# Unread products in the history stage of a recommender kernel, and a table moved to another PSUM bank

## The chip, the cores and the metric

The kernel runs on one core of a Trainium2 chip. Its metric is the device time of one execution in microseconds (us). A core has five engines with an instruction stream each: TensorE (PE in the rows, with PEld for its loads of the stationary operand), VectorE (DVE), ScalarE (ACT), GpSimd (POOL) and SyncE (SP). They meet only in semaphores: `then_inc` raises one, `wait_ge` holds an engine until one has reached a value.

## The reference

2048 examples have an item, a user and 100 users of a history. A row of a table has D = 128 numbers. The tables have 12500 and 62500 rows, and the ids are drawn from a wider range: an id past the end reads the last row, which is what most ids of the history do.

```python
items_emb = item_table[items]
user_emb = user_table[users]
hist_emb = user_table[history_users]
scores = einsum('bhd,bd->bh', hist_emb, user_emb)
user_his_emb = einsum('bh,bhd->bd', scores, hist_emb)
x = concatenate([items_emb, user_his_emb, user_emb], axis=1)   # 2048 x 384
x = dice(batchnorm(x @ W1 + b1, g1, be1), a1)                  # W1: 384 x 1024
x = dice(batchnorm(x @ W2 + b2, g2, be2), a2)                  # W2: 1024 x 512
return x @ W3 + b3                                             # W3: 512 x 1
```

Everything is in float32. A float32 product of 128x128 by 128x128 stands in the trace as two MATMUL records and two LDWEIGHTS records. A transpose is one of each.

## The kernel before

**Plan (0 to 45 us).** The 2048 examples are ordered by how many ids of their history are past the end, and cut into `TILES` = 16 tiles of 128 with about equal counts in a tile. `rank` holds each example's place in that order, one column per tile. Ids past the end need no gather: their count times the last row's score and the last row itself enter as one product. The ids left are gathered in slots: a slot is one row for each of the 128 examples of a tile. Four slots are a group (`GROUP` = 4), and a ring of 16 rows in SBUF holds four groups. `ends` holds the running count of slots. Examples are put in their order by products with matrices of zeros and ones ("places"), which VectorE builds by comparing `rank` with column numbers (`find_places`, L689, `find_own_places`, L697 and L702).

**History stage (45 to 838 us).** The four engines run the same loop over tiles and groups, each in its own stream:
- GpSimd gathers a group's four slots (L520, an indirect DMA each). Ahead of a group it waits for the indices (`idx_ready`) and for the place in the ring (`rows_free`). The arrival of a group is passed on to VectorE (`relay`) behind the third gather of the next.
- VectorE (`weigh`) multiplies the rows with the user's row (L812), sums over D (L818), masks the score (L822), and hands on the next indices (L827).
- ScalarE scales each slot's row by its score (`scale_rows`, L1236) into one of four buffers `scaled`. It waits for the scores of the group and, for each buffer, for TensorE's sum four slots before (`slot_summed`). The last scale of a group raises `rows_free`. Behind the loop over groups of a tile stands `keep_rows` (L1205), which waits for the placing product of two tiles ahead and copies it; then come the tile's last group and `pooled_T` (L1265). VectorE sorts a tile's ids out of what L1205 copied.
- TensorE sums the scaled rows in PSUM by products with the identity (`add_rows`, L1486), four a group, each waiting for its scale. Between groups it does other work of the tile, written out by hand: the last row's product (L1495), two transposes (L1502, L1503), `place_own` (L1423, L1428), `layer1_pooled` of the tile before (L1473), `place_keys` of two tiles ahead, the first half behind group 1 and the second behind the loop (L1407), and `layer1_own` (L1467), half behind group 2 and half behind group 3. The loop over the groups that are left (L1522) holds `add_rows` alone.

A tile has seven or eight groups: four ahead of the loop, two or three in it, one behind. A tile's order of work on TensorE is thus: last row, group 0, transposes, places, layer 1 of the tile before, group 1, places, group 2, half of layer 1, group 3, half of layer 1, rounds, the placing product, last group.

**Dense stage (838 to 1014 us).** Batchnorm, dice, W2, again batchnorm and dice, W3. TensorE is busy 95% of it.

`keep_busy` (L1453 to L1456) multiplies the identity by itself into the first 128 columns of PSUM bank 0, and nothing reads these. The kernel before calls it twice: 8 products ahead of the last tile's last group, and 20 behind the last `layer1_pooled`. `warm_up` (L1386) is the same in the plan.

Of the kernel before, what the change touches and what calls it, by code (L numbers as in the profile page):

```python
# [6 lines left out]
P = 128  # L7
# [31 lines left out]
def recommender_kernel(nc, items, users, history, item_table, user_table, W1, b1, g1, be1, a1,  # L39
# [6 lines left out]
    TILES = B // P  # L46
# [18 lines left out]
    BINS = HIGH - LOW + 1  # L65
# [7 lines left out]
    with ExitStack() as ctx:  # L73
# [153 lines left out]
        ps = ctx.enter_context(nc.psum_tensor("ps", [P, 8, 512], F32))  # L227
# [6 lines left out]
        ids_in = ps[:, 1, 64:64 + 2 * TILES]  # L234
        lasts = ps[:, 1, 96:96 + TILES]
        lasts_cut = ps[:, 1, 112:112 + TILES]
        rank = ps[:, 0, 2 * P:2 * P + TILES]
        rank_bins = ps[:, 1, 144:144 + TILES]
        same = ps[:, 1, 256:512].rearrange("p (t u) -> p t u", u=TILES)

# [146 lines left out]
        def hold(eng, semaphore, value):  # L387
            if not isinstance(value, int):
                eng.wait_ge(semaphore, value)  # L389
                eng.sem_inc(passed, 1)  # L390
            elif value > 0:
                eng.wait_ge(semaphore, value)

        def end_of(eng, t):

            return eng.value_load(ends[0:1, t + 1:t + 2], min_val=MIN_SLOTS * (t + 1), max_val=HIST * (t + 1))
# [977 lines left out]
        def _(pe):  # L1374
# [22 lines left out]
            def place_keys(t, j):  # L1397

                if t:
                    pe.wait_ge(places_found, 2 * t + 3 + j)  # L1400
                if j == 0 and t:
                    pe.wait_ge(tile_kept, t)
                    pe.wait_ge(whose_kept, t)
                for m in range(M1):
                    if t == 0 and m % 4 == 0:
                        pe.wait_ge(places_found, 2 * j + m // 4 + 1)
                    mm = nc.tensor.matmul(rows_ps, places[:, m, j, :], people[:, 2 * m + j, :],  # L1407
                                          start=(j == 0 and m == 0), stop=(j == 1 and m == M1 - 1), skip_group_check=True)
                if j == 1:
                    mm.then_inc(rows_placed, 1)  # L1410

            def place_own(i, t):

                pe.wait_ge(own_places_found[i], t + 1)
                if t == 0:
                    hold(pe, own_moved[i], own_more[i] + 1)
                elif i == 0:
                    pe.wait_ge(user_kept, t)
                    pe.wait_ge(item_set, t)
                of = own_ps[:, i * D:(i + 1) * D]  # L1420

                def first(s):
                    return nc.tensor.matmul(of, own_places[i][:, s, :], own_rows[i][:, s, :], start=(i == 0 and s == 0),  # L1423
                                            stop=(i == 1 and s == OWN_SLOTS - 1), skip_group_check=True)
                first(0)
                with pe.Fori(0, own_more[i]) as s:
                    hold(pe, more_found[i], own_more[i] * t + s + 1)
                    nc.tensor.matmul(of, more_places[i][:, :], own_rows[i][:, bass.ds(s + OWN_SLOTS, 1), :], start=False, stop=False,  # L1428
                                     skip_group_check=True).then_inc(more_used[i], 1)
                for s in range(1, OWN_SLOTS):  # L1430
                    mm = first(s)
                mm.then_inc(own_placed[i], 1)
# [20 lines left out]
            def keep_busy(count):  # L1453

                for _ in range(count):
                    nc.tensor.matmul(idle_ps, ident[:, :], ident[:, :], start=True, stop=True)  # L1456

            def layer1_own(t, blocks):


                if blocks.start == 0:
                    pe.wait_ge(both_kept, t + 1)
                if t:
                    pe.wait_ge(l1_kept, M1 * (t - 1) + blocks.stop)
                for m in blocks:
                    for k, of in ((0, P), (2, 0)):
                        nc.tensor.matmul(l1_ps[:, m, :], w1[:, k, m * P:(m + 1) * P], both_T[:, of:of + P],  # L1467
                                         start=(k == 0 and m == blocks.start), stop=False, skip_group_check=True)

            def layer1_pooled(t):  # L1470
                pe.wait_ge(pooled_kept, t + 1)
                for m in range(M1):
                    mm = nc.tensor.matmul(l1_ps[:, m, :], w1[:, 1, m * P:(m + 1) * P], pooled_T[:, :],  # L1473
                                          start=False, stop=True, skip_group_check=True)
                    if m % 4 == 3:
                        mm.then_inc(l1_done, 1)

            def add_rows(g, t, end):
                for j in range(GROUP):
                    if j < GROUP - 1:  # L1480
                        hold(pe, slot_scaled, g * (GROUP - 1) + (t * (GROUP - 1) + j + 1))
                    elif end:
                        pe.wait_ge(end_scaled, t + 1)
                    else:
                        hold(pe, rows_free, g + 1)
                    nc.tensor.matmul(pooled_ps, scaled[:, j, :], ident[:, :], start=False, stop=False,  # L1486
                                     skip_group_check=True).then_inc(slot_summed, 1)

            for t in range(TILES):
                begin.append(end_of(pe, t))  # L1490
                g0, g1 = begin[t] >> 2 if t else 0, begin[t + 1] >> 2
                pe.wait_ge(last_ready, t + 1)
                if t:
                    pe.wait_ge(pooled_kept, t)
                nc.tensor.matmul(pooled_ps, last_scaled[:, :], ident[:, :], start=True, stop=False,  # L1495
                                 skip_group_check=True)
                add_rows(g0, t, False)
                pe.wait_ge(user_kept, t + 1)
                pe.wait_ge(item_set, t + 1)
                if t:  # L1500
                    pe.wait_ge(both_kept, t)
                nc.tensor.transpose(turn_ps[:, 0:P], own[:, 0, :], ident[:, :])  # L1502
                nc.tensor.transpose(turn_ps[:, P:2 * P], own[:, 1, :], ident[:, :]).then_inc(turned, 1)  # L1503
                if t + 1 < TILES:
                    place_own(0, t + 1)
                if t:
                    layer1_pooled(t - 1)
                add_rows(g0 + 1, t, False)
                if t + 1 < TILES:
                    place_own(1, t + 1)  # L1510
                if t == 0:
                    place_keys(1, 0)
                    place_keys(1, 1)
                elif t + 2 < TILES:
                    place_keys(t + 2, 0)
                add_rows(g0 + 2, t, False)
                layer1_own(t, range(0, 4))
                add_rows(g0 + 3, t, False)
                if t == 0:
                    place_keys(2, 0)  # L1520
                layer1_own(t, range(4, M1))
                with pe.Fori(g0 + 4, g1) as g:  # L1522
                    add_rows(g, t, False)
                if t + 2 < TILES:
                    place_keys(t + 2, 1)
                if t == TILES - 1:
                    keep_busy(8)
                add_rows(g1, t, True)
                pe.wait_ge(slot_summed, g1 * GROUP + (t * GROUP + 2 * GROUP))
                pe.sem_inc(pooled, 1)  # L1530
# [181 lines left out]
```

## Time and profile before

| | |
|---|---|
| median of 3 runs | 1004.77 us (1000.77 to 1005.12) |
| the profiled execution | 1015.52 us, span 1013.7 us |
| busy in the span | TensorE 653.8, VectorE 522.8, GpSimd 495.0, ScalarE 360.5 us |
| gathers of history slots | 432 records (L520), 412.1 us |
| sums of scaled rows (L1486) | 984 records, 211.7 us |

The rows further down are of the profiled execution. A row of the timeline is one piece of work or several equal ones behind each other (x4); the bracket says how long the engine was idle ahead of it and what ended that. "issue" means that nothing in the profile was waited for; "remote" that the semaphore was raised by something the profile could not assign. The granted clock (PEclk) is TensorE's, as a share of its full 2.4 GHz, and has two levels, so 0.70 is a mixture of stretches at full and at half speed.

### The profile page before, as it was taken

The numbers are of one execution on the slowest core, as the hardware profiler recorded it, in microseconds if no ns is written. First come the engines' busy times: TensorE is split into PE (matmuls) and PEld (weight loads), VectorE is DVE, ScalarE is ACT, GpSimd is POOL, SyncE is SP. The second block draws the span as 40 slices with busy tenths as digits, with TensorE's granted clock in tenths as the row PEclk, the third lists the DMA queues.
The fourth block names the chain that finished last, engine by engine and source line by source line (L and its number), as shares of the span: only waits on it lengthen the run. The fifth ranks groups of instructions, "written<-read, shape, count | busy, mean of one in ns | idle before, by whom it ended". The sixth has DMA issues, their size and how long they took to land.

```text
span 1013.7 us, 17230 instructions
## 1 busy us (share of the span) xinstructions
PE 653.8 (64%) x3753; PEld 606.6 (60%) x3753; DVE 522.8 (52%) x1353; ACT 360.5 (36%) x884; POOL 495.0 (49%) x561
## 2 busy tenths in 40 slices
PE   4563665637473846566566475756665569999998
PEld 3552555537373736465566364745664469888887
DVE  7653444344353625353445254544434536999758
ACT  3122232322231414132223142332233247787556
POOL 6655544545455453636354635545544524290036
PEclk8676776767587666767677667768777779999999
DMA  7111111111111111111111111111111110000000
GB/s 215 40 38 39 37 34 35 37 37 37 37 35 39 30 44 25 44 27 44 30 40 32 44 26 39 36 32 39 38 34 35 42 22 1 2 1 0 1 1 2
DMA packets 17241, 34.65 MB, mean 34 GB/s; under 512 B 8104, under 2 KB 8400, under 8 KB 17168
## 3 DMA queue, kind: packets, MB, share of 16 engines
q0 software_dynamic: 14208, 29.13, 11.7%
q1 hardware_dynamic: 2960, 4.67, 1.4%
q8 instruction: 32, 0.52, 0.2%
q14 instruction: 41, 0.34, 0.1%
HBM read 33.76 MB, written 0.01 MB: 33 GB/s over the span
## 4 chain that ended last, share of the span: by engine, by line
PE 45%; another core or an unknown queue 19%; issue 18%; ACTq 8%; ACT 6%; DVE 3%; DVEq 0%; PEldq 0%; POOL 0%; POOLq 0%
PE ps L1486 14%; PE ps L1544 10%; PE ps L1407 6%; PE ps L1423 5%; ACTq L1236 3%; ACT scaled L1236 3%; PE ps L1473 3%; ACTq L1257 2%; PE ps L1495 1%; ACTq L389 1%; ACTq L390 1%; PE ps L1559 1%; PE ps L1428 1%; PE ps L1386 1%
## 5 line engine op out<-in xcount | busy, mean ns | idle before, releaser
L520 POOL DMA_INDIRECT rows<-in_L_rec_user_table_dram,slot_idx x432 | 412.1, 954 | 388.3 <-ACT scaled L1236 260.6
L1486 PE MATMUL ps<-ident,scaled 128*128 128x128 f32 x984 | 211.7, 381 | 225.8 <-ACT scaled L1236 171.9
L1486 PEld LDWEIGHTS ps<-ident,scaled 128*128 128x128 f32 x984 | 186.8, 278 | 249.4 <-issue 221.8
L1236 ACT ACTIVATE scaled<-rows,work 128x128 f32 (+1 forms) x492 | 176.5, 401 | 271.5 <-remote 191.1
L812 DVE TENSOR_TENSOR prod<-rows,ps 128x512 f32<-128x512 f32 x122 | 83.7, 686 | 168.4 <-POOLq L527 88.1
L689 DVE SCALAR_TENSOR_TENSOR h<-ps,col_no 128x1024 f32<-128x1024 f32 (+1 forms) x34 | 39.2, 1161 | 159.0 <-ACT ranked L1205 88.1
L1544 PE MATMUL ps<-h,w 128*128 128x256 f32 (+1 forms) x576 | 113.3, 356 | 1.0 <-DVE h L1042 1.0
L1407 PE MATMUL ps<-wide,h 128*128 128x104 f32 x512 | 98.6, 369 | 14.6 <-issue 14.6
L1544 PEld LDWEIGHTS ps<-h,w 128*128 128x128 f32 x576 | 99.6, 190 | 12.8 <-issue 1.2
L1407 PEld LDWEIGHTS ps<-wide,h 128*128 128x128 f32 x512 | 94.3, 281 | 21.2 <-issue 21.2
L818 DVE TENSOR_REDUCE work<-prod 128x512 f32 (+1 forms) x122 | 83.7, 686 | 38.8 <-issue 25.5
L1467 PE MATMUL ps<-both_T,w 128*128 128x128 f32 x512 | 72.2, 292 | 22.7 <-issue 22.7
L1467 PEld LDWEIGHTS ps<-both_T,w 128*128 128x128 f32 x512 | 67.6, 209 | 18.3 <-issue 18.1
L1224 ACT ACTIVATE h<-ps,par 128x128 f32<-128x128 f32 x128 | 36.4, 372 | 106.0 <-remote 103.6
L1423 PE MATMUL ps<-wide,work 128*128 128x128 f32 x160 | 33.2, 306 | 41.2 <-issue 41.2
L1205 ACT ACTIVATE ranked<-ps 128x104 f32<-128x104 f32 x16 | 4.1, 258 | 138.3 <-remote 114.2
L1423 PEld LDWEIGHTS ps<-wide,work 128*128 128x128 f32 x160 | 26.3, 215 | 40.3 <-issue 40.1
L556 POOL TENSOR_SCALAR h<-h,scale,shift 128x256 f32<-128x256 f32 (+1 forms) x29 | 22.2, 779 | 49.4 <-DVE h L1042 28.8
L822 DVE SCALAR_TENSOR_TENSOR work<-wide,ends_f,work (+1 forms) x122 | 27.2, 223 | 33.9 <-issue 16.4
L1423 PE MATMUL ps<-wide 128*128 128x128 f32 x160 | 34.1, 364 | 4.8 <-DVE wide L697 4.8
L1423 PEld LDWEIGHTS ps<-wide 128*128 128x128 f32 x160 | 32.2, 285 | 4.9 <-issue 4.9
L1473 PE MATMUL ps<-pooled_T,w 128*128 128x128 f32 x256 | 33.3, 286 | 0.5 <-ACT pooled_T L1265 0.5
(217 smaller groups left out, 784.7 us busy)
## 6 DMA issues: line engine op xcount, KB each, us to landing
rows<-in_L_rec_user_table_dram,slot_idx POOLq DMA_INDIRECT x432
w<-in_L_rec_W_dram SPq DMA_DIRECT2D x1, 2048.0 KB, 17.5
w<-in_L_rec_W_dram SPq DMA_DIRECT2D x1, 1536.0 KB
h<-in_r_history_users_dram SPq DMA_DIRECT2D x2, 400.0 KB, 3.4
wide<-in_L_rec_user_table_dram,own_idx POOLq DMA_INDIRECT x5
wide<-in_L_rec_item_table_dram,own_idx POOLq DMA_INDIRECT x5
last_row<-in_L_rec_user_table_dram SPq DMA_DIRECT2D x1, 64.0 KB
last_item<-in_L_rec_item_table_dram SPq DMA_DIRECT2D x1, 64.0 KB
```

The source lines that it names most:

```text
L520: nc.gpsimd.indirect_dma_start(rows[:, s, :], None, user_table, bass.IndirectOffsetOnAxis(slot_idx[:, s:s + 1], 0)).then_inc(landed[s], 16)
L689: nc.vector.scalar_tensor_tensor(places[:, of, j, :], rank.rearrange("p (m j) -> p m j", j=2)[:, of, j].unsqueeze(2).to_broadcast(shape), ...
L812: nc.vector.tensor_tensor(prod[:, :, :], rows[:, at, :], user_now.unsqueeze(1).to_broadcast([P, GROUP, D]), ALU.mult).then_inc(multiplied, 1)
L818: nc.vector.tensor_reduce(raw[:, pair], prod[:, :, :], AX_X, ALU.add).then_inc(dotted, 1)
L1224: nc.scalar.activation(h1[:, m, t * P:(t + 1) * P], l1_ps[:, m, :], ACT.Identity, bias=b1c[:, m:m + 1]).then_inc(l1_kept, 1)
L1236: nc.scalar.activation(scaled[:, j, :], rows[:, bass.ds((g & (GROUPS - 1)) * GROUP + j, 1), :], ACT.Copy, scale=score[:, bass.ds(g * GROUP ...
L1407: mm = nc.tensor.matmul(rows_ps, places[:, m, j, :], people[:, 2 * m + j, :], start=(j == 0 and m == 0), stop=(j == 1 and m == M1 - 1), sk ...
L1423: return nc.tensor.matmul(of, own_places[i][:, s, :], own_rows[i][:, s, :], start=(i == 0 and s == 0), stop=(i == 1 and s == OWN_SLOTS - 1 ...
L1467: nc.tensor.matmul(l1_ps[:, m, :], w1[:, k, m * P:(m + 1) * P], both_T[:, of:of + P], start=(k == 0 and m == blocks.start), stop=False, sk ...
L1473: mm = nc.tensor.matmul(l1_ps[:, m, :], w1[:, 1, m * P:(m + 1) * P], pooled_T[:, :], start=False, stop=True, skip_group_check=True)
L1486: nc.tensor.matmul(pooled_ps, scaled[:, j, :], ident[:, :], start=False, stop=False, skip_group_check=True).then_inc(slot_summed, 1)
L1544: mm = nc.tensor.matmul(l2_ps[c % 2][:, o, 0:w], w2[:, k, o * P:(o + 1) * P], h1[:, k, chunk(c)], start=(k == 0), stop=(k == M1 - 1))
```

## The change

Two things. The rank columns move from PSUM bank 0 (columns 256 to 271) to bank 4, behind the table `in_bin`; they are written and read by the same VectorE instructions as before. And TensorE gets unread products (`keep_busy`): 40 in a loop of its own ahead of the first tile's first product, 4 behind each half of `layer1_own` in each tile, 10 in each round of the loop over groups, and 4 behind the placing product in the tiles that have one there.

```diff
--- before.py
+++ after.py
@@ -234,7 +234,7 @@
         ids_in = ps[:, 1, 64:64 + 2 * TILES]
         lasts = ps[:, 1, 96:96 + TILES]
         lasts_cut = ps[:, 1, 112:112 + TILES]
-        rank = ps[:, 0, 2 * P:2 * P + TILES]
+        rank = ps[:, 4, BINS * TILES:(BINS + 1) * TILES]
         rank_bins = ps[:, 1, 144:144 + TILES]
         same = ps[:, 1, 256:512].rearrange("p (t u) -> p t u", u=TILES)
 
@@ -1486,9 +1486,16 @@
                     nc.tensor.matmul(pooled_ps, scaled[:, j, :], ident[:, :], start=False, stop=False,
                                      skip_group_check=True).then_inc(slot_summed, 1)
 
+
+
+            BETWEEN = 4
+            IN_LOOP = 10
             for t in range(TILES):
                 begin.append(end_of(pe, t))
                 g0, g1 = begin[t] >> 2 if t else 0, begin[t + 1] >> 2
+                if t == 0:
+                    with pe.Fori(0, 10):
+                        keep_busy(4)
                 pe.wait_ge(last_ready, t + 1)
                 if t:
                     pe.wait_ge(pooled_kept, t)
@@ -1515,14 +1522,18 @@
                     place_keys(t + 2, 0)
                 add_rows(g0 + 2, t, False)
                 layer1_own(t, range(0, 4))
+                keep_busy(BETWEEN)
                 add_rows(g0 + 3, t, False)
                 if t == 0:
                     place_keys(2, 0)
                 layer1_own(t, range(4, M1))
+                keep_busy(BETWEEN)
                 with pe.Fori(g0 + 4, g1) as g:
                     add_rows(g, t, False)
+                    keep_busy(IN_LOOP)
                 if t + 2 < TILES:
                     place_keys(t + 2, 1)
+                    keep_busy(BETWEEN)
                 if t == TILES - 1:
                     keep_busy(8)
                 add_rows(g1, t, True)
```

The first place is TensorE's stream where the history stage begins; `ends` is the load of the tile's end, `last_scaled` the last row times its weight. Before:

```order
L1423 MATMUL ps<-wide,work 128x128 x4
L396 TENSOR_LOAD ends [waits w1_loaded,plan_ready]
L396 ISA x2
L1495 MATMUL ps<-ident,last_scaled 128x128 [waits last_ready]
L1486 MATMUL ps<-ident,scaled 128x128 [waits slot_scaled] x3
L1486 MATMUL ps<-ident,scaled 128x128 [waits rows_free]
L1502 MATMUL ps<-ident,own 128x128 [waits item_set,user_kept]
```

The same stretch now:

```order
L396 TENSOR_LOAD ends [waits w1_loaded,plan_ready]
L396 ISA x2
L1497 UNCONDITIONAL_BRANCH
L1456 MATMUL ps<-ident 128x128 x4
L1497 REGISTER_ALU
L1497 COMPARE_AND_BRANCH
L1502 MATMUL ps<-ident,last_scaled 128x128 [waits last_ready]
L1486 MATMUL ps<-ident,scaled 128x128 [waits slot_scaled] x3
```

Ten rounds of four products stand between the load of `ends` and the wait for the last row (L1495 before is L1502 now).

The second place is the loop over groups and what follows it, in TensorE's stream; `h1` in L1407 holds the places of the second half. Before:

```order
L1467 MATMUL ps<-both_T,w1 128x128 x8
L1522 UNCONDITIONAL_BRANCH
L1522 ISA
L1486 MATMUL ps<-ident,scaled 128x128 [waits slot_scaled]
L389 REGISTER_ALU
...
L1486 MATMUL ps<-ident,scaled 128x128 [waits rows_free]
L1522 ISA
L1522 COMPARE_AND_BRANCH
L1407 MATMUL ps<-wide,h1 128x104 [waits places_found]
L1407 MATMUL ps<-wide,h1 128x104 x7
```

The same stretch now (L1531 is the loop's line):

```order
L1467 MATMUL ps<-both_T,w1 128x128 x8
L1456 MATMUL ps<-ident 128x128 x4
L1531 UNCONDITIONAL_BRANCH
L1531 ISA
...
L1486 MATMUL ps<-ident,scaled 128x128 [waits rows_free]
L1456 MATMUL ps<-ident 128x128 x10
L1531 ISA
L1531 COMPARE_AND_BRANCH
L1407 MATMUL ps<-wide,h1 128x104 [waits places_found]
L1407 MATMUL ps<-wide,h1 128x104 x7
L1456 MATMUL ps<-ident 128x128 x4
```

Each product here is two loads and two products in the engine's stream. The loop's round grows by ten products behind its four sums, and four more stand on either side of the loop and its placing product. The streams of the other engines are as before.

## Rows read from the trace of the kernel before

**Rows 1.** Windows of the two stages: start:end, length, busy of PE, PEld, DVE, ACT, POOL, clock, DMA, GB/s.
```profile
45.00:838.00 793.00, 467.38 (x2656) 438.18 (x2655) 348.58 (x1020) 228.32 (x689) 399.92 (x421) 0.70 0.14 36
838.00:1014.00 176.00, 167.16 (x998) 150.44 (x998) 144.00 (x241) 121.77 (x171) 65.67 (x89) 0.99 0.00 1
```
**Rows 2.** The page's chain of waits by engine, shares of the span.
```profile
PE 45%; another core or an unknown queue 19%; issue 18%; ACTq 8%; ACT 6%; DVE 3%; DVEq 0%; PEldq 0%; POOL 0%; POOLq 0%
```
**Rows 3.** List of waits: engine, line, waited for, us in total, times, longest.
```profile
POOL rows L520 <- ACT scaled L1236: 260.6, 48, 9.1
ACT scaled L1236 <- remote: 191.1, 38, 10.1
...
ACT ranked L1205 <- remote: 114.2, 13, 11.7
```
**Rows 4.** The page's costliest groups: busy us, mean ns, idle before.
```profile
L1486 PE MATMUL ps<-ident,scaled 128*128 128x128 f32 x984 | 211.7, 381 | 225.8 <-ACT scaled L1236 171.9
```
**Rows 5.** Timeline of 305 to 336 us: start, duration, engine, line, count, idle before.
```profile
306.01 0.95 POOL L520 DMA_INDIRECT rows<-in_L_rec_user_table_dram,slot_idx  x1 [0.30 <-issue]
...
309.23 1.44 ACT L1236 ACTIVATE scaled<-rows,work 128x128 f32 x4 [10.10 <-remote]
...
309.78 4.92 PE L1486 MATMUL ps<-ident,scaled 128*128 128x128 f32 x20 [7.02 <-ACT scaled L1236]
311.09 1.44 ACT L1236 ACTIVATE scaled<-rows,work 128x128 f32 x4 [0.42 <-PE ps L1486]
311.48 0.95 POOL L520 DMA_INDIRECT rows<-in_L_rec_user_table_dram,slot_idx  x1 [4.51 <-ACT scaled L1236]
...
317.87 0.46 PE L1486 MATMUL ps<-ident,scaled 128*128 128x128 f32 x2 [2.46 <-issue]
...
318.17 3.62 PE L1407 MATMUL ps<-wide,h 128*128 128x104 f32 x16
...
325.23 0.95 POOL L520 DMA_INDIRECT rows<-in_L_rec_user_table_dram,slot_idx  x1 [0.30 <-issue]
328.82 0.26 ACT L1205 ACTIVATE ranked<-ps 128x104 f32<-128x104 f32 x1 [11.09 <-remote]
...
329.98 2.05 PE L1486 MATMUL ps<-ident,scaled 128*128 128x128 f32 x8 [8.20 <-ACT scaled L1236]
```
**Rows 6.** Timeline of 286 to 298 us, TensorE.
```profile
291.30 0.25 PE L1407 MATMUL ps<-wide,h 128*128 128x104 f32 x1 [1.18 <-issue]
```
**Rows 7.** Windows of the three bursts of the tile, columns as in rows 1.
```profile
282.50:289.90 7.40, 6.63 (x53) 6.58 (x51) 5.12 (x18) 1.89 (x5) 5.88 (x6) 0.89 0.18 44
297.30:308.50 11.20, 5.45 (x47) 5.26 (x45) 5.53 (x16) 1.64 (x5) 7.53 (x8) 0.96 0.19 48
311.50:327.70 16.20, 7.56 (x34) 6.71 (x33) 2.89 (x9) 2.58 (x7) 11.32 (x12) 0.71 0.19 49
```
**Rows 8.** Chain of waits near 840 us, unread products of the kernel before.
```profile
840.19 4.47 PE ps L1456 x40
```
**Rows 9.** Timeline of the plan and the first tile.
```profile
10.62 4.33 PE L1386 MATMUL ps<-not_before,ident 128*128 128x128 f32 x20 [3.51 <-issue]
...
44.63 0.80 PE L1495 MATMUL ps<-ident,last_scaled 128*128 128x128 f32 x2 [5.85 <-issue]
...
49.35 1.92 PE L1423 MATMUL ps<-wide 128*128 128x128 f32 x8
...
58.38 0.38 ACT L1252 ACTIVATE both_T<-ps 128x256 f32<-128x256 f32 x1 [11.36 <-remote]
```
**Rows 10.** Timeline of 660 to 682 us, a tile with two rounds.
```profile
666.85 1.93 PE L1407 MATMUL ps<-wide,h 128*128 128x104 f32 x16
...
672.36 0.26 ACT L1205 ACTIVATE ranked<-ps 128x104 f32<-128x104 f32 x1 [6.12 <-remote]
```
**Rows 11.** Timeline of 826 to 842 us, TensorE in the last tile.
```profile
830.50 1.06 PE L1486 MATMUL ps<-ident,scaled 128*128 128x128 f32 x8
...
837.19 0.49 PE L1486 MATMUL ps<-ident,scaled 128*128 128x128 f32 x2 [0.33 <-ACT scaled L1236]
```

## Prediction

> **What bounds the kernel now.** I read the windows of the two stages first [rows 1]. The history stage (45 to 838 us) holds 793 of the span's 1013.7 us, and every engine is idle for much of it: TensorE is busy 467 us, GpSimd 400, the other two less, at a mean granted clock of 0.70, against 0.99 in the dense stage. A stage with 326 us of TensorE idle looks as if it had room for filler, and as if a warmer clock could pay. Whether it does is in the waits.
>
> The chain of the whole span [rows 2] gives TensorE 45%, but a fifth to a wait that the profile can't name and 18% to "issue", where an engine waits for nothing that shows. The list of waits [rows 3] says who stands: GpSimd waits 260.6 us in 48 stretches for ScalarE to free gathered rows, and ScalarE stands "remote" 191.1 us ahead of scaling and 114.2 us ahead of keeping the placed rows (L1205). The sums (L1486) are 984 records at 381 ns [rows 4]; they wait for ScalarE for 172 us. So TensorE waits for ScalarE, and ScalarE is not waiting for TensorE most of the time.
>
> The timeline of the tile from 280 to 333 us shows the cycle [rows 5]. GpSimd's burst of gathers ends at 306.96; ScalarE resumes at 309.23 after 10.10 us; its fourth scale lets GpSimd start 12 gathers at 311.48, which end at 326.18; ScalarE does L1205 only at 328.82, though TensorE had finished the placing product it needs at 318.17 + 3.62 = 321.79. The 7 us between have no producer: ScalarE comes back 2.3 and 2.6 us after the bursts. In bursts the issue of instructions is slow on other engines too: TensorE at 291.30 does a single record of 0.25 us behind 1.18 us of idle that nothing accounts for [rows 6]. That burst began at 282.5, and TensorE had had 53 products' records and 51 weight loads by 289.9 [rows 7]. My reading: while gathers are issued, an engine can draw on some hundred instructions that it already holds, and then gets one in about 0.7 us until about 2 us after the burst. The end of a tile is set by burst plus recovery, not by arithmetic on TensorE.
>
> **The change, part by part.**
> The rank columns move to another bank. The same VectorE instruction reads the same 16 columns; the bank it leaves is the one that unread products write. Cost 0.
>
> The unread products: 40 ahead of tile 0; 4 + 4 in each of 16 tiles (128); 4 after the placing product in 14 tiles (56); 10 in each loop round. The stage has 984/8 = 123 groups [rows 4] (a product is two records), of which each tile takes four ahead of the loop and one behind it, so 123 - 80 = 43 rounds and 430 products. Together 654 products, 1308 records. Prices: at full clock 40 records took 4.47 us, 0.112 each [rows 8]; at half clock 20 took 4.33, 0.217 each [rows 9]. So 146 us of TensorE if warm, 283 if cold, into 326 idle.
>
> *Front.* TensorE is idle for 5.85 us ahead of 44.63 [rows 9]; the 40 products start near 39 and take 80 x 0.112 = 9.0 us, to 48; cold 17.3, to 56. What follows ends at 49.35 + 1.92 = 51.27 before [rows 9], with the first sums, transposes and places 6.6 us long from 44.63; it would end near 55 (63 cold). ScalarE takes the transposes only at 58.38, and TensorE's next sums wait behind that. Warm they are hidden: 0; cold, up to +5. I take 0, since the 4 us before are products as well.
>
> *Parts and rounds of a tile with three rounds.* Before, TensorE does 20 records at 309.78, the last product of that group at 317.87, places 318.17 to 321.79, and idles 8.20 us to 329.98 [rows 5]. After: first group to 311.5; ten products, mostly still cold, 4.0 to 315.5; second group, now warm, 0.9 to 316.4; ten products 2.2 to 318.6; third group 0.9 to 319.5; ten products 2.2 to 321.7; places 1.8 to 323.5 (the price warm is 16 records in 1.93 us [rows 10]); four products to 324.4. ScalarE's four scales of the second group keep their place, those of the third wait for the second's sums, some 2.5 us later, but GpSimd needs them only for its ninth gather, at 311.48 + 8 x 1.25 = 321.48 (twelve take 14.70). The placed rows are read at 328.82, so 5.3 us of slack stay: 0 if TensorE is fed. If it is not, see the second rival.
>
> *Tiles with two rounds* (about five). Places end at 668.78 before, ScalarE reads at 672.36 [rows 10]. Twenty products (4.2) make that 673.0: +0.6 on the read. The waits of 2 us and more behind a burst can take that up; I take 0, at most +3 over all.
>
> *4 + 4 between parts.* 1.8 us a tile, in a burst where TensorE holds 47 + 45 records [rows 7] and then waits for ScalarE 7.02 us [rows 5]: 0; with the slow issue it can push the rest 2.5 us later, still inside that wait.
>
> *Last tile.* Here the chain runs on TensorE: sums and layer 1 follow each other from 830.50, the last sum stands at 837.19 with 0.33 us of idle before it [rows 11]. Four, four and one round's ten are 18 products = 36 x 0.112 = 4.0 us, less some 0.5 of idle: +3.5.
>
> *What a warm clock gives back.* Eight records at 329.98 take 2.05 us [rows 5]; eight at full clock took 1.06 [rows 11]. A tile ends with four such sums, ScalarE 0.3 behind each: at best 0.7 us a tile. ScalarE's two stands of 0.42 us for the ring [rows 5] could go too, about 1.5 us in all and 23 over 15 tiles. But TensorE still has 324.4 to 329.98 idle before exactly these sums, 5.6 us instead of 8.20. In this trace the clock at 309.78 was half after 7.02 us of idle. I take nothing for most tiles, -0.7 in a few: -1.
>
> The Trainium skill, "TensorE: Matmul & The Clock Gate", section on HAM oscillation, says that waits between bursts of products return the clock to half and each burst starts cold again. By that rule the gaps of 5 to 8 us that stay would keep the sums cold, and only gaps that are closed would pay, which is the third case below at its full -23. This trace agrees as far as it goes (2.05 us after 8.20 of idle); it has no row with 5.6.
>
> Sum: 0 + 0 + 0 + 3.5 - 1, about +3. The profiled execution took 1015.5 us (span 1013.7 and 1.8 around it), so 1018; the median of the runs is 1004.8, and 3 on top gives 1008.
>
> **The rivals.**
> *B, slower: TensorE runs out of instructions it holds.* Place: the 12-gather burst of three-round tiles. Before, TensorE had 34 + 33 records in it [rows 7], below the 104 at which it went slow in the burst at 282.5. After, three times ten products add up to 60 + 60, the loop's body grows from 28 instructions to 68, and four products follow. It decides if the count passes some 110 before the placing product is done: then TensorE gets through the rest only from about 328, when the burst is over. About ten unread products at half clock (4.33) and places (3.62) stand there: 335.9 instead of 328.82, +7.1 for ScalarE's L1205 and all behind it, in ten tiles +71. With the last tile's 3.5: 1080. If every branch costs such a stop, it is more; if a loop's body is held once it has been run, nothing. For it: [rows 6]; against: in the burst at 311.48 TensorE came out of the loop's last sum at 317.87 and began the placing product at 318.17, with no stop behind the branch [rows 5], though with the short body.
>
> The Trainium skill, "Runtime: NRT & Kernel Launch", Instruction fetch mechanics, says that fetching ahead is sequential and that a taken branch out of the pages held stops the engine for a fetch. By that rule a longer body is likelier to cross a page and stop in each of 43 rounds. No row here shows such a stop on TensorE.
>
> *C, faster: the clock stays up and the sums shrink.* -23 from above, with +3.5 in the last tile partly won back: about 983. For it: a clock of 0.70 over 793 us [rows 1], and sums that stand on the chain. Against: ScalarE's return, which no product moves.
>
> *D, a little slower:* no stop, but the covers are thinner than I think: front cold +5, 0.6 to 1.5 us in each tile: +15 to +30, about 1025. Its sign is that places end within 1 us of L1205.
>
> *That it does nothing*, since idle of 5.6 us is as cold as 8.2, is part of the first case.
>
> **How the numbers follow.** Hidden and near nothing 0.45 (own range 997 to 1013); B 0.25; C 0.20; D 0.10. The likeliest is 1008. The range reaches down into C and up to B's own price: 975 to 1085. What can be told from no change here is 0.5%, 5 us. Faster: C's 0.20 and 0.10 of the first case. Same: 0.25 of the first case. Slower: B, D and 0.10 of the first case, 0.45.
>
> **What would show it.** In the profile after: TensorE's busy time up by 146 to 283 us and nothing else changed in the stage; ScalarE's L1205 still about 2.6 us after GpSimd's last gather; GpSimd's 48 waits near 260 us; the clock of the stage above 0.80; the sums at 329.98 still near 2 us for eight; the last tile 3.5 us longer. B would show as single records 0.7 us or more apart in the unread products, and L1205 following the placing product at once. C would show as eight records near 1.1 us at the end of tiles, and tile starts 1 to 2 us closer. I am wrong in the mechanism if the tiles get shorter or longer by over 1 us each while L1205 still follows the burst.

## The result and the profile after

The changed kernel took 1049.82 us (median of 4 runs, 1045.7 to 1051.38) against 1004.3 us before on the same chip: ratio 1.0433, 95% interval 1.0405 to 1.0461, so 45.5 us slower. The forecast was 1008 with a range of 975 to 1085. The time is in the range, but the likeliest case, no change, was wrong.

One thing has to be known before the experiments are read. They ran on several chips, and these are of two kinds. On the first (the two runs above, and experiments 1 to 4) the kernel before takes 1003 to 1004 us. On the second (all later ones, on four other chips) the very same program takes 751 us. No chip is known to be in both groups, and the second group ran later. That the chip makes the difference, and not something else that changed in between, is therefore the nearest reading and not shown; "kind of chip" below stands for it. Each run is given as a ratio to the kernel before on its own chip.

Windows of the changed kernel's two stages (start:end, length, busy of PE, PEld, DVE, ACT, POOL, clock, DMA share, GB/s), against [rows 1]:

```profile
45.00:870.00 825.00, 604.00 (x3894) 571.82 (x3894) 347.69 (x1017) 224.71 (x686) 401.28 (x420) 0.81 0.14 34
870.00:1049.00 179.00, 170.71 (x1030) 153.69 (x1028) 144.09 (x241) 121.93 (x171) 65.62 (x89) 1.00 0.00 1
```

The products and the clock did what was said: TensorE has 1238 records more in the history stage, 137 us more of busy time, and a mean clock of 0.81 instead of 0.70. The other engines do the same work in 32 us more. The list of waits, against [rows 3]:

```profile
ACT scaled L1236 <- remote: 321.1, 43, 11.0
POOL rows L520 <- ACT scaled L1236: 297.7, 62, 12.8
DVE h L689 <- ACT ranked L1205: 205.8, 14, 15.5
ACT ranked L1205 <- PE ps L1407: 134.7, 16, 11.6
```

GpSimd stands 62 times for ScalarE instead of 48: there are 14 stands more. Eight of them are long: gathers are over 2 us apart in 56 places instead of 48, and none of the nine bursts of 12 gathers is left. ScalarE now waits ahead of L1205 for TensorE's placing product all 16 times; before, 13 of the 16 waits had no producer that the profile could name. The sums themselves got cheaper, 183.9 us instead of 211.7 [rows 4], and the unread products took 217.6:

```profile
L1456 PE MATMUL ps<-ident 128*128 128x128 f32 x1364 | 217.6, 316 | 58.7 <-issue 58.2
L1486 PE MATMUL ps<-ident,scaled 128*128 128x128 f32 x984 | 183.9, 343 | 53.7 <-ACT scaled L1236 48.9
```

The chain of the page, where [rows 2] had TensorE at 45%:

```profile
PE 60%; issue 17%; another core or an unknown queue 13%; ACT 4%; DVE 4%; ACTq 1%; DVEq 0%; PEldq 0%
```

Where the time went, by the first product of each tile in the two profiled executions: tile 0 begins 18.3 us later (62.9 against 44.6), tile 1 only 10.4 us later (126.3 against 115.9); from there the tiles add 0.4 to 2.5 us each up to tile 14, which takes 6.0 us more; the rest adds 1.5. The profiled execution of the kernel before was some 10 us above its median and that of the changed one 1.6, so about 0.6 us a tile has to be added in thought.

The front, in the timeline of the changed kernel (start, duration, engine, line, count, idle before; of this and the later timelines only the rows that the text needs are shown):

```profile
37.52 4.72 PE L1456 MATMUL ps<-ident 128*128 128x128 f32 x39
44.10 0.27 PE L1456 MATMUL ps<-ident 128*128 128x128 f32 x1 [1.85 <-issue]
44.83 0.37 PE L1456 MATMUL ps<-ident 128*128 128x128 f32 x1 [0.46 <-issue]
46.94 0.37 PE L1456 MATMUL ps<-ident 128*128 128x128 f32 x1 [1.74 <-issue]
49.07 0.37 PE L1456 MATMUL ps<-ident 128*128 128x128 f32 x1 [1.76 <-issue]
...
53.00 0.94 POOL L520 DMA_INDIRECT rows<-in_L_rec_user_table_dram,slot_idx  x1 [0.30 <-issue]
...
56.75 6.27 PE L1456 MATMUL ps<-ident 128*128 128x128 f32 x35 [2.43 <-issue]
62.86 0.39 PE L1502 MATMUL ps<-ident,last_scaled 128*128 128x128 f32 x2
```

TensorE does 39 of the 80 records at full speed and then gets one in 0.7 to 2.8 us. GpSimd's burst ends at 53.94, and the last 35 records start 2.8 us behind that, at half clock (0.50 up to 61 us, 0.90 in the 2 us after). That is slow issue as in [rows 6], here in a loop of four products: a loop's body that has been run four times over is starved too.

And a tile's end in the changed kernel, against [rows 5]:

```profile
333.76 0.35 PE L1456 MATMUL ps<-ident 128*128 128x128 f32 x1 [0.98 <-issue]
...
335.19 0.35 PE L1456 MATMUL ps<-ident 128*128 128x128 f32 x1 [1.08 <-issue]
...
338.40 1.44 ACT L1236 ACTIVATE scaled<-rows,work 128x128 f32 x4 [9.47 <-remote]
338.95 2.05 PE L1486 MATMUL ps<-ident,scaled 128*128 128x128 f32 x8 [0.17 <-ACT scaled L1236]
340.65 0.94 POOL L520 DMA_INDIRECT rows<-in_L_rec_user_table_dram,slot_idx  x1 [4.34 <-ACT scaled L1236]
340.79 4.27 PE L1456 MATMUL ps<-ident 128*128 128x128 f32 x20
...
344.89 1.93 PE L1407 MATMUL ps<-wide,h 128*128 128x104 f32 x16
346.66 1.08 PE L1456 MATMUL ps<-ident 128*128 128x128 f32 x8
346.86 0.26 ACT L1205 ACTIVATE ranked<-ps 128x104 f32<-128x104 f32 x1 [7.02 <-PE ps L1407]
...
348.03 1.45 PE L1486 MATMUL ps<-ident,scaled 128*128 128x128 f32 x8 [0.29 <-ACT scaled L1236]
```

The burst that held 12 gathers has become one of 8 and one of 4, with a stand of 4.34 us between them. L1205 follows the placing product within 0.05 us, and that follows the round's ten unread products, which ran at half clock.

### The profile page after: what moved, and what is told of

It is laid out like the page before. It is cut to its first block, busy times and chain, and to the rows that moved or that the text cites. A ratio compares the mean times of both kernels' runs of the same rounds, so it can differ in the third digit from the quotient of the medians.

```text
span 1049.6 us, 19867 instructions
## 1 busy us (share of the span) xinstructions
PE 798.6 (76%) x5061; PEld 747.9 (71%) x5061; DVE 523.4 (50%) x1353; ACT 357.8 (34%) x884; POOL 497.2 (47%) x561
## 4 chain that ended last, share of the span: by engine, by line
PE 60%; issue 17%; another core or an unknown queue 13%; ACT 4%; DVE 4%; ACTq 1%; DVEq 0%; PEldq 0%
PE ps L1486 13%; PE ps L1456 13%; PE ps L1555 10%; PE ps L1407 7%; PE ps L1467 6%; PE ps L1423 3%; PE ps L1473 2%; ACT scaled L1236 2%; PE ps L1570 1%; ACTq L1236 1%; PE ps L1428 1%; PE ps L1653 1%; PE ps L1502 1%; PE ps L1639 1%
## 5 line engine op out<-in xcount | busy, mean ns | idle before, releaser
L1456 PE MATMUL ps<-ident 128*128 128x128 f32 x1364 | 217.6, 316 | 58.7 <-issue 58.2
L1456 PEld LDWEIGHTS ps<-ident 128*128 128x128 f32 x1364 | 204.2, 231 | 68.0 <-issue 67.9
L1486 PE MATMUL ps<-ident,scaled 128*128 128x128 f32 x984 | 183.9, 343 | 53.7 <-ACT scaled L1236 48.9
L1486 PEld LDWEIGHTS ps<-ident,scaled 128*128 128x128 f32 x984 | 164.4, 246 | 68.0 <-issue 64.9
L1407 PE MATMUL ps<-wide,h 128*128 128x104 f32 x512 | 84.4, 305 | 49.0 <-issue 48.7
L1407 PEld LDWEIGHTS ps<-wide,h 128*128 128x128 f32 x512 | 75.9, 218 | 55.6 <-issue 55.5
L1467 PE MATMUL ps<-both_T,w 128*128 128x128 f32 x512 | 81.5, 310 | 28.8 <-issue 28.5
L1467 PEld LDWEIGHTS ps<-both_T,w 128*128 128x128 f32 x512 | 75.0, 225 | 29.0 <-issue 28.8
L1205 ACT ACTIVATE ranked<-ps 128x104 f32<-128x104 f32 x16 | 4.1, 257 | 134.7 <-PE ps L1407 134.7
L1423 PE MATMUL ps<-wide,work 128*128 128x128 f32 x160 | 27.3, 290 | 14.8 <-issue 14.8
L1423 PE MATMUL ps<-wide 128*128 128x128 f32 x160 | 29.5, 326 | 4.8 <-DVE wide L697 4.8
```

## The experiments

Two theories were put against each other. Theory T, for time: unread products stand between two groups' sums, ScalarE gets its four buffers back later, and that late return is what costs. Theory I, for instructions: each instruction more in a burst of gathers brings TensorE nearer to the point at which it is starved of them.

**1. The front alone.** The 40 products ahead of tile 0 stay, the other added ones go.

```diff
-                keep_busy(BETWEEN)
...
-                    keep_busy(IN_LOOP)
```
(`keep_busy(BETWEEN)` goes in all three places.)

> Only the 40 products ahead of tile 0 (and the rank columns in bank 4). In the changed kernel the first tile's first product came at 62.9 us instead of 44.6, but the second tile only 10.4 us later than before. Theory I (the products are starved of instructions while GpSimd gathers): the same start near 63 us, and +8 to +12 us on the whole kernel, near 1014. Theory T (the loss of the change sits in the loop rounds, and the late start is taken up by waits that stand anyway): less than +5 us.

Measured: 1006.0 us, ratio 1.0021 (1.0004 to 1.0039): +2.8 us by the medians. The start moved as in the whole change, to 62.0 us, but tile 1 began at 120.3, only 4.4 us behind. Of 17 us of delay the next tile gives 13 back: ScalarE and GpSimd had stands of their own there. The guess of 8 to 12, taken from the changed kernel's start of tile 1, was too high, and theory T's "less than +5" held.

**2. The products between the parts alone.**

```diff
-                if t == 0:
-                    with pe.Fori(0, 10):
-                        keep_busy(4)
...
-                    keep_busy(IN_LOOP)
```

> Only the groups of 4 products between a tile's parts and behind the placing product. Theory I: each burst of 8 gathers has TensorE at 100 to 110 instructions already, 16 more in the third and fourth part push it into slow issue: +3 to +8 us. Theory T: 0.9 to 1.8 us of TensorE's time a tile beside its waits, only the last tile pays: +2 us. A warmer clock that pays would show as -5 or less.

Measured: 1007.47 us, ratio 1.0042 (1.0023 to 1.0062), +4.2 us. The interval is +2.3 to +6.2 us, so it lies in theory I's range (+3 to +8) and a little above theory T's +2: it tells them apart only weakly. There is no gain by the clock, though its mean from 45 to 830 us was 0.75.

The trace of this run bears on what follows. In four of its tiles, those that begin at 118.72, 384.31, 435.90 and 533.94 us, the burst of 12 gathers broke into 8 and 4, and these tiles took 51.5 to 52.0 us. The same tiles took 52.1 to 52.2 us in experiment 1, with the burst whole. So a broken burst need not cost anything by itself.

**3. The loop rounds' products alone.** As 1 and 2, with only `keep_busy(IN_LOOP)` left.

> Only the 10 products in each loop round. Theory T (they stand ahead of the next group's sums, so ScalarE gets its scale buffers back 1 to 2.5 us later, its third group slips behind the burst, and the 12-gather burst splits into 8 and 4 with one more stand of 4.3 us): four bursts in three-round tiles, +20 to +27 us. Theory I (loop rounds run out of instructions): the same size, but with L1205 waiting for a placing product that comes in single records 0.7 us apart.

Measured: 1035.57 us, ratio 1.0301 (1.0273 to 1.0330), +32.3 us: most of the loss. The three parts alone sum to 39.3 of 45.5. Neither theory's +20 to +27 us held it. Rows of the timeline, in the tile from 342 to 396 us, show what an unread product does in a round:

```profile
372.35 1.44 ACT L1236 ACTIVATE scaled<-rows,work 128x128 f32 x4 [0.42 <-issue]
372.71 3.90 PE L1456 MATMUL ps<-ident 128*128 128x128 f32 x20
372.73 0.94 POOL L520 DMA_INDIRECT rows<-in_L_rec_user_table_dram,slot_idx  x1 [3.54 <-ACT scaled L1236]
376.45 1.06 PE L1486 MATMUL ps<-ident,scaled 128*128 128x128 f32 x8
377.34 2.40 PE L1456 MATMUL ps<-ident 128*128 128x128 f32 x20
383.01 0.40 ACT L1236 ACTIVATE scaled<-rows,work 128x128 f32 x1 [9.21 <-remote]
...
386.28 0.94 POOL L520 DMA_INDIRECT rows<-in_L_rec_user_table_dram,slot_idx  x1 [3.86 <-ACT scaled L1236]
```

ScalarE has scaled a group by 373.79 and has no buffer left. (The first 20 records belong to the round before, the second 20 to this one.) TensorE, instead of summing it at once, does ten unread products (3.90 us, cold). The sums start at 376.45, 3.7 us into the burst, and ScalarE's next scale comes at 383.01, after the burst. The kernel of experiment 1, with no products there, is at the same point in another state:

```profile
310.19 5.02 PE L1486 MATMUL ps<-ident,scaled 128*128 128x128 f32 x20 [1.31 <-ACT scaled L1236]
...
311.56 1.44 ACT L1236 ACTIVATE scaled<-rows,work 128x128 f32 x4 [0.42 <-issue]
311.95 0.94 POOL L520 DMA_INDIRECT rows<-in_L_rec_user_table_dram,slot_idx  x1 [3.57 <-ACT scaled L1236]
313.42 1.17 ACT L1236 ACTIVATE scaled<-rows,work 128x128 f32 x3 [0.42 <-PE ps L1486]
316.28 0.40 ACT L1236 ACTIVATE scaled<-rows,work 128x128 f32 x1 [1.68 <-issue]
```

Here ScalarE scales four more slots behind the start of the burst, the first three 1.5 us into it, and the group is free for GpSimd's ninth gather. That is theory T's sign, and the list of waits fits it: GpSimd stands for ScalarE 48 times before, 49 and 52 times in experiments 1 and 2, and 61 times here.

Theory I's sign, the placing product in single records, isn't in this tile, where the product runs in one piece from 390.08 to 392.01. It is in others. The stage has 14 tiles with a placing product. In the eight whose burst broke, it ran in one piece. In five of the other six it came in pieces with nothing waited for between them, though the unread products just ahead of it had run through. Here is a tile with two rounds, to be held against [rows 10]:

```profile
726.18 2.40 PE L1456 MATMUL ps<-ident 128*128 128x128 f32 x20
728.41 1.65 PE L1407 MATMUL ps<-wide,h 128*128 128x104 f32 x11
...
730.53 0.55 PE L1407 MATMUL ps<-wide,h 128*128 128x104 f32 x3 [0.47 <-issue]
730.77 0.94 POOL L520 DMA_INDIRECT rows<-in_L_rec_user_table_dram,slot_idx  x1 [0.30 <-issue]
731.92 0.37 PE L1407 MATMUL ps<-wide,h 128*128 128x104 f32 x2 [0.84 <-issue]
733.61 0.26 ACT L1205 ACTIVATE ranked<-ps 128x104 f32<-128x104 f32 x1 [10.52 <-PE ps L1407]
```

In [rows 10] the placing product ended at 668.78, ScalarE read it at 672.36, and the burst of gathers went on to 674.88: ScalarE took its turn inside the burst. Here the product ends at 732.29 and the burst at 731.71, and ScalarE reads at 733.61, behind both.

The lengths of the tiles in the profiled executions say how much each kind of tile lost, experiment 3 against experiment 1. The seven tiles behind the first one in which 12 gathers became 8 and 4 are 7.3 us longer together. The tile from 174 us, where 12 and 4 became 8 and 8, is 3.9 us longer. The five tiles with two rounds, in which no burst broke, are 10.5 us longer. The last tile but one, which has no placing product, is 6.2 us longer: there ScalarE had begun its last four scales inside the burst (793.80 in experiment 1), and now it does them behind it (826.51). So most of the loss is not in the broken bursts.

**4. The same instructions, 8 columns wide.**

```diff
-                    nc.tensor.matmul(idle_ps, ident[:, :], ident[:, :], start=True, stop=True)
+                    nc.tensor.matmul(idle_ps[:, 0:cols], ident[:, :], ident[:, 0:cols], start=True, stop=True)
```
(`cols` is 8 in each added call, 128 in the calls that were there before.)

> The changed kernel with each added product 8 columns wide instead of 128: as many instructions, little TensorE time, so the bursts of the clock may differ too. Theory I: the instruction count decides, so nearly all of the +45 us stays: 1035 to 1050. Theory T: the loop's part goes and only the starved front stays: 1010 to 1022.

Measured: 1099.49 us, ratio 1.0938 (1.0909 to 1.0968). Neither theory had this, since both took a narrow product to be short. It isn't. The windows of its history stage, and its added products:

```profile
45.00:916.00 871.00, 713.19 (x3854) 694.77 (x3854) 346.03 (x1012) 224.56 (x682) 400.38 (x421) 0.65 0.13 33
```
```profile
L1456 PEld LDWEIGHTS ps<-ident 128*128 128x128 f32 x1364 | 273.1, 302 | 23.4 <-issue 23.2
L1456 PE MATMUL ps<-ident 128*128 128x8 f32 x1308 | 258.4, 332 | 24.3 <-issue 24.3
```

A record takes 332 ns in the mean, where it took 316 in the whole change. At the same half clock the two widths take the same time, ten products of 8 columns here against 4.27 us for ten of 128 columns at 340.79 in the changed kernel:

```profile
342.02 4.28 PE L1456 MATMUL ps<-ident 128*128 128x8 f32 x20
```

The weight load of 128x128 is in both, and probably sets the time; no run changed it. The granted clock was 0.65 instead of 0.81, below the 0.70 of before. So the run tests something else: the same number of instructions at a lower clock costs 96 us instead of 45. The count alone does not set the loss, then. By this comparison, the warmer clock of the real change wins back about half of what its products would cost without it.

**5 to 8, on chips of the second kind.** Experiment 5 is the rank columns alone, 6 is 14 products behind the placing product, 7 has all the rounds' products ahead of the loop, 8 the front written out as `keep_busy(40)`. Numbers 6 to 8 have the rank columns moved and no other unread products added. Number 7 against the kernel before:

```diff
+                with pe.Fori(g0 + 4, g1) as g:
+                    keep_busy(IN_LOOP)
                 with pe.Fori(g0 + 4, g1) as g:
                     add_rows(g, t, False)
```

> The kernel before with only the rank columns moved to bank 4, no product added. Both theories: no difference, within 0.3%. Its profile is also a second look at the kernel before, whose profiled execution took some 10 us more than its median: if this one does not, part of what I compared per tile (52.7 us each) was that one execution's.

> The rank columns moved, and 14 unread products behind the placing product of 14 tiles, in the 5 to 8 us in which TensorE waits for ScalarE's return; nothing ahead of the loop's sums. They take 3.1 us warm, up to 6.1 cold. Theory T (the loss comes from work ahead of the sums): no loss, and the sums of the tile's end at a warm clock, so -5 to -12 us. Theory I (each instruction more in a burst is paid): TensorE goes slow and is still in them when ScalarE resumes: +5 to +20.

> As the run with the loop's products alone (+32 us), with the same 430 products, but all rounds' products in a loop of their own ahead of the loop of sums, so none stands between two groups' sums. Theory T (ScalarE gets its buffers late because unread products stand between the sums, and misses the burst): the 12-gather bursts stay whole, +0 to +10. Theory I (starvation): 120 instructions more in the second burst, which holds 92 records already, so the products run into slow issue and past ScalarE's return: +40 to +80.

> The 40 products ahead of tile 0 written out without a loop (and the rank columns moved). If the loop's branch is what starves TensorE there, they run through in 9 us and the first product is at 45 to 49 us. If the count of instructions in a burst decides, TensorE stops after about as many records as with the loop (35 and then single ones 1.4 to 2.8 us apart), and the first product is again near 62.

Measured, against 751.38 us: rank columns 751.16, ratio 1.0001 (0.9991 to 1.0011); 14 behind 751.45, 1.0003 (0.9994 to 1.0013); ahead of the loop 755.29, 1.0058 (1.0041 to 1.0075); front written out 751.08, 0.9997 (0.9986 to 1.0007). The rank columns cost nothing. The other three were aimed at slow issue, and this chip shows none of it: in number 8 the 80 records of the front ran through in 9.10 us beside gathers. So they could not tell T from I. What bounds the kernel there is in its windows and waits (the kernel with the rank columns moved):

```profile
40.00:550.00 510.00, 379.15 (x2538) 359.69 (x2538) 330.41 (x973) 216.58 (x653) 385.04 (x406) 0.80 0.22 53
```
```profile
ACT scaled L1236 <- DVE work L822: 133.6, 55, 5.2
PE ps L1486 <- ACT scaled L1236: 118.0, 64, 4.6
POOL rows L520 <- issue: 112.8, 370, 0.3
```

GpSimd's gathers follow each other: 406 in 510 us, 1.25 us each. None waits over 0.3 us for ScalarE or with nothing to wait for; six wait up to 1.3 us for their indices. No "remote" stands in ScalarE's first place any more; it waits for VectorE's scores, by name. The gather itself takes 951 ns here and 954 before.

**9 and 10. The change itself on a chip of the second kind, and number 7 again.**

> The changed kernel once more. The last four runs were on a chip on which the kernel before takes 751 us, not 1003: other engines issue at their usual pace while GpSimd gathers, and gathers follow each other without stands. If this call gets such a chip, theory T/I (both rest on slow issue in bursts and on ScalarE's late return) say that most of the +4.5% goes: GpSimd's gathers are the bound there, 1.25 us each, and the loop's products are hidden beside them; only the last tile's 4 us and a little stay, +4 to +9 us on 751. A rival says that the products between the sums cost the same 45 us on any chip. If it is a chip of the first kind, +42 to +48 us on 1003 again.

> The 430 products of the loop rounds in a loop ahead of the sums (and the rank columns moved). On a chip of the second kind it took +0.6% already and will again. On one of the first kind: theory T (unread products between the sums hold ScalarE's buffers) +0 to +10 us on 1003; theory I (starvation by the count of instructions in a burst) +40 to +80.

Measured: the change 753.09 us against 751.52, ratio 1.0017 (1.0008 to 1.0027), +1.6 us, less than the +4 to +9 expected; number 7 again 755.57, 1.0049 (1.0032 to 1.0065). The change costs 45 us on one kind of chip and 1.6 on the other, with the same instructions. Its front and its history windows there:

```profile
33.51 9.62 PE L1456 MATMUL ps<-ident 128*128 128x128 f32 x80
42.97 0.39 PE L1502 MATMUL ps<-ident,last_scaled 128*128 128x128 f32 x2
```
```profile
40.00:550.00 510.00, 466.81 (x3759) 451.67 (x3757) 330.66 (x972) 216.29 (x653) 385.27 (x405) 0.96 0.21 53
```

The 80 records run through in 9.62 us, gathers or not. The clock is 0.96 and TensorE busy 92% of the window, and GpSimd does the same gathers in the same time: TensorE has that much room.

**11. The whole change with the rounds' products ahead of the loop.**

> The changed kernel whole, but with the loop rounds' products in a loop of their own ahead of the loop of sums. Against 1.043 for the change on a chip of the first kind: theory T says the loop's +32 us go and 1.010 stays (front and parts, +2.8 and +4.2 us, and the last tile's 4); theory I says it gets worse, 1.05 to 1.09. On a chip of the second kind, where the change took 1.002 and these products ahead of the loop alone 1.005 to 1.006: 1.005 to 1.009.

Measured, again on the second kind: 757.65 us, ratio 1.0069 (1.0052 to 1.0086), as expected for it. Up to thirty products in one piece ahead of the loop cost more there than ten in each round (1.0017). Why was not followed up.

**12. Twelve ahead of the loop and fourteen behind the placing product.**

```diff
+                keep_busy(12)
                 with pe.Fori(g0 + 4, g1) as g:
                     add_rows(g, t, False)
                 if t + 2 < TILES:
                     place_keys(t + 2, 1)
+                    keep_busy(14)
```

> 12 unread products ahead of each tile's loop of sums and 14 behind its placing product, 388 in all, nearly as many as in the loop rounds (430), and none between two groups' sums. On a chip of the first kind (1003 us before): theory T says that ScalarE's buffers come free as before, so no more than +8 us, or a gain of up to 10 by the warmer clock; theory I says that 388 products cost about what 430 did, +25 to +35. On a chip of the second kind (751.5): 14 behind took nothing and 430 ahead took 4 us, so 0 to +3.

Measured, on the second kind: 751.27 us, ratio 0.9999 (0.9990 to 1.0007). 388 products at a tile's two idle places are free there, with a clock of 0.92 over the execution, and bring nothing: the bound is GpSimd's. No kernel tried beat the one before on either kind of chip.

## Why the prediction was right and wrong

The range held the time only because rival B's price, 1080, stood in it. For the case called likeliest that is luck: 1008 was forecast, with its own range up to 1013, and 1049.8 measured. That case failed in how it treated the rounds.

- *Rank columns, 0.* Right: 1.0001.
- *Front, hidden, the products done by 48.* The size was nearly right (+2.8 us) and the way was wrong. I priced 80 records by TensorE's rate of 0.112 us and did not count them as instructions in a burst, though the text had just read slow issue from [rows 6] and [rows 7]. They ended at 63.0. The cover, GpSimd's and ScalarE's own stands in tile 0, was there all the same.
- *Parts, 0, and the last tile, +3.5.* Measured +4.2 for all products between the parts, which are 8 of the last tile's 18. The expected place was off: the last tile and the dense stage were 1.5 us longer in the whole change, and the tile before it 6.0, of which the loop's products alone (experiment 3) make 5.9. That tile had no term of its own.
- *Rounds, 0, in tiles with three and with two of them.* This is the failed step; the rounds' products measured +32.3. For three rounds it is the sentence "ScalarE's four scales of the second group keep their place, those of the third wait for the second's sums, some 2.5 us later, but GpSimd needs them only for its ninth gather". The wait for the sums was there (ten products took 3.90 us cold), but it is not a shift by 2.5 us that followed. ScalarE's next scale came behind the burst (383.01 in experiment 3, 6 us after the sum that made room for it), the burst broke into 8 and 4, and the placing product came late too. The 5.3 us of slack had been measured from a placing product that starts in the same burst. Yet the seven tiles of this kind lost only 7.3 us in experiment 3.
- *The two-round tiles were mis-sized more.* The forecast was +0.6 us on the read, taken as 0, at most +3 over all. The sum was also low: by its own 0.112 us a record twenty products take 4.5 us and not 4.2, which gives +0.9. In the kernel before ScalarE reads at 38.1 to 38.3 us into such a tile, inside the burst; in experiment 3 it reads at 41.3 to 42.3 us, behind the burst, and the five tiles lost 10.5 us. The prediction took ScalarE's return as something "which no product moves". The rows say otherwise: ScalarE gets some work done inside a burst, and where TensorE's sums or placing product are late for that turn, the work waits until the burst is over.
- *Rival B, TensorE runs out of held instructions in the rounds, +7 in ten tiles.* Both of its signs came, single records and L1205 behind the placing product. Its cause came in part. In the whole change a round's unread products can end in single records, in the tile shown above from 333.76 to 338.8. With the rounds' products alone, which is most of the loss, the unread products run nearly through, and it is the placing product of the tiles with two rounds that comes in pieces. Between the first tile and the last two, no tile lost more than about 4 us against experiment 1, in place of the 7 forecast. So the 1080 was right only as an upper end.
- *The branch.* The Trainium skill, "Runtime: NRT & Kernel Launch", Instruction fetch mechanics, has a taken branch stop an engine if its target is not among the pages held. The front shows no such stop: on chips of the second kind its 80 records took 9.62 us in a loop of ten rounds and 9.10 written out (experiment 8). That is 0.05 us a round at most, since the loop also began at a mean clock of 0.63 in its first 1.5 us and the other at 1.00. A loop this short may never leave the pages held, so this is no test of the rule.
- *The third case, a warmer clock pays.* The clock rose as its sign said, to 0.81, and the sums lost 28 us of busy time. They did not shorten the kernel: experiment 2, with 0.75 and nothing in the rounds, was still 4.2 us slower. By experiment 4 the clock is worth about 50 us to a stream with that many added products, that is, it pays back part of what the products cost.

What is shown: the split by parts, which tiles lose, that a burst can break without a loss, and that the loss is there where issue is slow (+45 us) and nearly absent where it is not (+1.6 us). What is read from traces and not tested: that ScalarE misses its turn inside the burst because TensorE's sums or placing product come later, and how much of that lateness is the time of the unread products and how much is slow issue. The experiments that would have parted the two (numbers 7 and 12) fell on chips without slow issue. A version with eight scale buffers, which would take the buffer wait away, was not tried.

What makes the two kinds of chips differ stays open. The program, the number of gathers and the time of each are the same, and so are the packets on the two queues that the page calls "instruction": 32 and 41 in the kernel before, and 32 and 41 in experiment 5.

## What to carry to other kernels

An engine that is idle is not free: ask what stands behind the filler on its own engine, who waits for that, and whether that engine can still act a few us later. By this reading filler belongs behind the last thing somebody waits for, not between two such things; no run tried that alone where issue is slow. Before tuning to stands that end with no producer, see whether the same program has them on another chip.

## What the runs showed of the hardware

- In one group of runs TensorE got a record only every 0.7 to 2.8 us while GpSimd issued indirect gathers, after the first 39 of the front's 80, and until 2.8 us behind the burst; a loop of four products did not escape it. In the other group the same 80 records ran through in 9.62 us beside gathers, and the kernel before took 751 us instead of 1003.
- A float32 product with 8 columns took as long as one with 128 at the same half clock (ten of them 4.28 and 4.27 us), and the stage's clock stayed lower with it (0.65 against 0.81).
